# Repeated score passes in head 0's first waits, counting matmuls four steps later, scatters placed 32 score groups later, last stores from two queues

## The reference

```
xn = layernorm(x)
q, k, v = xn @ Wq.T, xn @ Wk.T, xn @ Wv.T          # 16 heads of 16
attn    = softmax(q k^T / sqrt(256)) @ v
rw      = softmax(xn @ gate_w.T), kept for the 2 best of 8 experts (by scores + gate_b)
expert(t) = silu((t @ w1 + b1) * (t @ w3 + b3)) @ w2 + b2      # hidden size 352
out = x + attn + sum_e rw[e] * expert_e(xn) + expert_shared(xn)
```

## Time and profile before

| | |
|---|---|
| three timed runs | 2171.87, 2173.07, 2174.39 us, median 2173.07 |
| the profiled execution | 2174.21 us, of which the span is 2172.3 us |
| busy in the span | PE 99%, ACT 93%, DVE 37%, POOL 11% |
| chain that ended last | PE 92%, ACT 7%, DVE 1% |
| mean granted PE clock | 0.996 of full speed |

### The profile page before, as it was taken

One profiled execution on the slowest core, in us unless ns is written; L12 is line 12 of the kernel. 1 busy time (PEld: TensorE's weight loads), 2 busy tenths in 40 slices (PEclk: granted clock), 3 DMA queues, 4 the chain that ended last, 5 costly groups with the idle time before them and its releaser, 6 DMA issues.

```text
span 2172.3 us, 37982 instructions
## 1 busy us (share of the span) xinstructions
PE 2152.4 (99%) x15638; PEld 965.2 (44%) x15638; DVE 800.5 (37%) x1515; ACT 2009.4 (93%) x2209; POOL 246.0 (11%) x242
## 2 busy tenths in 40 slices
PE   9999999999999999999999999999999999999998
PEld 4632344444444444444444444444444444444322
DVE  6321143344344334334334434334334334544200
ACT  4599999999999999999999999999999999999998
POOL 0100465610000000000000000000000002223200
PEclk9999999999999999999999999999999999999999
DMA  7671334332222222213132222213213222332120
GB/s 254 206 280 33 91 121 130 100 90 66 63 78 63 76 57 79 78 54 85 48 77 70 77 64 69 78 50 83 75 50 90 63 69 75 105 97 66 57 78 3
DMA packets 223595, 187.24 MB, mean 86 GB/s; under 512 B 112039, under 2 KB 194558, under 8 KB 223166
## 3 DMA queue, kind: packets, MB, share of 16 engines
q1 hardware_dynamic: 211598, 149.41, 24.3%
q0 software_dynamic: 11824, 35.40, 5.0%
HBM read 130.21 MB, written 54.53 MB: 85 GB/s over the span
## 4 chain that ended last, share of the span: by engine, by line
PE 92%; ACT 7%; DVE 1%; DMA 0%; issue 0%; DVEq 0%
PE PS L672 41%; PE PS L659 29%; PE PS L684 12%; ACT probs L866 6%; PE PS L695 6%; PE PS L565 2%; PE PS L602 1%; PE PS L575 0%; DVE stats L972 0%; PE PS L554 0%; DMA resid<-in_x 0%; DVE probs L996 0%; ACT probs L818 0%; DVE o_t L1169 0%; DVE mv L975 0%
## 5 line engine op out<-in xcount | busy, mean ns | idle before, releaser
L866 ACT ACTIVATE probs<-PS 128x1024 f32<-128x1024 f32 x2048 | 1920.0, 1080 | 96.0 <-PE PS L659 81.8
L672 PE MATMUL PS<-probs,v_head 128*32 128x512 f32 x8192 | 1002.8, 601 | 1.1 <-ACT probs L866 0.8
L659 PE MATMUL PS<-q_ring,k_stack 50*128 50x512 f32 x4096 | 741.3, 446 | 7.0 <-ACT probs L866 6.2
L659 PEld LDWEIGHTS PS<-q_ring,k_stack 50*128 50x128 f32 x4096 | 332.6, 185 | 627.2 <-ACT probs L866 569.6
L672 PEld LDWEIGHTS PS<-probs,v_head 128*32 128x32 f32 x8192 | 206.6, 108 | 448.2 <-issue 359.6
L1194 DVE TENSOR_SCALAR gate_in<-PS,bias_sb 128x256 f32<-128x256 f32 x165 | 79.6, 482 | 754.9 <-PE PS L684 739.5
L684 PE MATMUL PS<-x_hi,w_hi 128*128 128x256 f32 (+1 forms) x660 | 201.3, 305 | 0.0
L684 PE MATMUL PS<-x_hi,w_lo 128*128 128x256 f32 (+1 forms) x660 | 186.5, 283 | 0.0
L684 PE MATMUL PS<-x_lo,w_hi 128*128 128x256 f32 (+1 forms) x660 | 185.6, 281 | 0.0
L921 POOL DMA_DIRECT2D slot_y<-y_sb x39 | 27.9, 716 | 1285.1 <-DVE y_sb L1262 1251.6
L684 PEld LDWEIGHTS PS<-x_hi,w_hi 128*128 128x128 f32 (+1 forms) x660 | 118.6, 180 | 60.0 <-issue 60.0
(11 more groups left out here) (137 smaller groups left out, 1098.2 us busy)
## 6 DMA issues: line engine op xcount, KB each, us to landing
w_raw<-in_w SPq DMA_DIRECT2D x110, 352.0 KB
k_stack<-qk_parts SPq DMA_DIRECT2D x120, 128.0 KB
w_raw<-in_w SPq DMA_DIRECT2D x55, 256.0 KB
q_ring<-qk_parts SPq DMA_DIRECT2D x384, 32.0 KB
slot_x<-part_a SPq DMA_DIRECT2D x39, 256.0 KB, 2.3
slot_in<-slot_x SPq DMA_DIRECT2D x156, 64.0 KB, 2.4
slot_y<-y_sb POOLq DMA_DIRECT2D x39, 256.0 KB, 2.5
k_stack<-qk_parts SPq DMA_DIRECT2D x136, 64.0 KB
```

The costliest lines, as they stand in the source:

```text
L659: last = pe.matmul(bank(2 * score_buffer(turn, g) + r), k_stack[rows, kt * P:(kt + 1) * P], q_ring[rows, sweep, i * QC:(i + 1) * QC], star ...
L672: last = pe.matmul(bank(O_BANK)[VW * j:VW * (j + 1), :], v_head[:, kt, :], probs[:, slot, (j % 2) * QC:(j % 2 + 1) * QC], start=(kt == 0), ...
L866: nc.scalar.activation(probs[:, prob_slot(g), :], bank(2 * score_buffer(h, g), 2), ACT.Exp, scale=ENERGY_SCALE).then_inc(s_exp, 1)
```

## The change

Four edits. (1) `filler(count)` repeats the first score matmuls of head 0 into banks 6 and 7, whose content nobody reads then; seven such pairs stand between the first score groups. The order of the real score groups and `values` is as before. (2) The counting matmuls stand in step 24 of head 0, not 20. (3) `scatter(u)` waits for `s_scores` at 128 + 32 + 8u, not 128 + 10u. (4) Of the last four stores, two are issued by ACT.

```
-                for c in range(sweep * QCH, (sweep + 1) * QCH):
+                for c in range(sweep * QCH, (sweep + 1) * QCH - 2 * sweep):
...
                 for k in range(1, GS + 1):
+                    if h == 0 and k == 1:
+                        continue
                     next_scores(2)
-                    if h == 0 and k == 20:
+                    if h == 0 and k == 24:
...
+            def filler(count):
+
+                for n in range(count):
+                    for r in range(2):
+                        rows = slice(r * HALF, r * HALF + ROWS)
+                        pe.matmul(bank(F_BANK + r), k_stack[rows, 0:P], q_ring[rows, 0, 0:QC], start=True, stop=True)
+
             next_scores(SB)
+            filler(3)
+            next_scores(1)
+            filler(2)
+            next_scores(1)
+            filler(2)
+            next_values(1)
             plain_head(0)
...
+            act.wait_ge(s_resid, SH + SWEEPS)
+            for c in range(NCH - 2, NCH):
+                nc.scalar.dma_start(out_v[:, c * TPC:(c + 1) * TPC, D - HD:D], resid[:, c * TPC:(c + 1) * TPC, D - HD:D]).then_inc(s_out, 16)
...
                 if u >= 2:
                     pool.wait_ge(s_scat[u % 2], 16 * TPU * TOP * (u // 2))
-                pool.wait_ge(s_scores, GH + 10 * u)
+                pool.wait_ge(s_scores, GH + 32 + 8 * u)
```

## The result

The changed kernel takes 2187.97 us (median of 5 runs, 2186.32 to 2189.01) against 2174.39 us of the kernel before (5 runs, timed beside it): ratio 1.0064, interval 1.0053 to 1.0075. Forecast was 2187.7, counted as 14.6 us over the median of 2173.07 that the kernel before had in its first three runs. The loss is 13.6 us, and the two profiled spans differ by as much (2185.9 against 2172.3).

The account below looks back on a forecast made before the run. PE was taken to bound heads 1 to 14, ACT heads 0 and 15. Edits 1 to 4: -1.8 + 0 + 17.4 - 1.0 = +14.6 us, giving 2187.7 us against the median 2173.07; 8-in-10 range 2176 to 2199.

Parts of the forecast that it names:

- The bound and the reading of POOL: Heads 0 and 15 go at ACT's pace, heads 1 to 14 at PE's; POOL's chain is held by its own work.
- the sharing: Split of the token-wait loss: unit 4 0, unit 5 7.7 us, unit 6 another 7.9, unit 7 nothing more; total 15.6.
- The start: POOL's first scatter, waiting for count 160, starts at 266.5 us instead of 234.03, 32.5 us later.
- Landing: Time a token load of POOL needs to land after its issue: 3.8 us, from 3.0 to 7.5.
- The free lateness: Between DVE's and PE's first use of a unit's tokens, 1.25 us of lateness costs nothing.
- The clock: PE leaves unit 6's token wait with its clock down: +1.8 us; the fall at unit 5 is swallowed.
- the rule of the Trainium skill: Long idle gaps between matmul bursts return PE to half clock; by it both forecast stands, units 5 and 6, bring a fall.
- The fall at 256.5 us: PE clock fall in the profile before, costing ACT 1.76 us; may come or go, left to the range.
- The rival of "another phase": The clock fall around 257 us may come or go, 1.8 us each way; in every range, no chance of its own.
- The chain that catches up: POOL's chain is quicker, 162 us to unit 6's load; -2.8 us, 2170.3; 0.14, shared with POOL being misread.
- The longer chain: POOL's chain gains no 4.4 us and a second clock fall adds 1.8: 2193.9 us; chance 0.20.
- the rule by which both stands' falls are paid in full: Clock falls after the stands at units 5 and 6 both paid: the term would be twice 1.8 us; no chance given.

Follow-up runs that it names:

- the run with the stands filled: Changed kernel plus identity matmuls ahead of up_both(u, 0) of units 4, 5, 6; 2185.49 us against 2170.55 us of the kernel before, ratio 1.0071.

## Why the prediction was right, and where its terms were not

**The bound and the reading of POOL: right.** POOL waited for a score count once (`L904` before, `L923` after), its chain moved as a block, and PE lost in the mixed heads what it waited there.

**Edit 3: right in mechanism and sum (+17.4 forecast, 18.2 in the ledger), by terms that were each a little off.**
- The chain from the first scatter to unit 6's load was to shrink by 4.4 us from 182.2; it shrank by 3.2, to 179.0. The wait of 6.80 us did go (2.37 in its place), and over the 14 scatters POOL waited 4.1 us less for its loads (49.5 against 53.6). But its normalisations and indirect DMAs took 0.9 us more, which the sum didn't have.
- Therefore the sharing was off. Up to unit 4's load the chain had shrunk by 0.5 us only (100.6 to 100.1), where the sum gave it all of the 4.4 at once. Unit 4 was forecast to lose nothing; measured from unit 3's, its split came 4.9 us late and PE stood for 3.22 us. That the total doesn't depend on the sharing, since the last late load sets it, held.
- The start: 262.66 us, with PE 4.4 us ahead of the profile before, is 267.0 on that profile's clock, against 266.5. Landing: 3.2 us for unit 6's load against 3.8.
- The free lateness: 1.25 us counted, 1.1 there. Unit 6's split is 18.0 us late (13.6 and the 4.4 of lead), but PE uses it 1.29 us after it begins instead of 2.38, so PE starts the unit 16.9 us late. The sum had 15.6.
- The clock: +1.8 forecast for the last stand, 1.3 measured: from PE's first use of unit 6's tokens to unit 7's split it was 30.09 us (433.64 to 463.73) and is 31.37 (446.18 to 477.55). So 16.9 + 1.3 = 18.2 stands against 15.6 + 1.8 = 17.4.
- The clock was down behind all three stands, the shortest of which had PE idle for 3.22 us. That is as the rule of the Trainium skill said it would be behind each stand ("TensorE: Matmul & The Clock Gate", "Why this matters for your kernels"). But in the run with the stands filled it fell behind 2.79 us of idle and not behind 3.08.
- That threshold steps of 8 groups don't hold the chain, and that SP's queue would be late without cost: both held. `load_slots(8)` went out at 468.19 us (471.8 forecast), and unit 8's split came 32.33 us after unit 7's. It held also where PE had not slipped: DVE waited 2.74 and 6.85 us for the weights, PE not at all.

**Edit 1: the fall was avoided, the gain isn't shown.** ACT's 1.81 us of idle are gone from the profile. Over all profiles taken, the clock fell at the start in two of two without the passes and in one of twelve with them. That speaks for the passes, though two is few. But the price of 1.8 was read from one profile: in the other without passes (only the new thresholds) the same fall cost ACT 0.61 us. In the medians edit 1 is worth 0.9 us, with an interval from 3.5 us quicker to 0.4 slower: the forecast of 1.8 is inside, and so is nothing.

**The fall at 256.5 us came out in my favour.** It is not in the profile after; by it PE's lead grows from 2.5 us in unit 0 to 4.6 at unit 1's split, 2.1 us, and ACT began head 0 0.5 us sooner. Together with the first fall that is the 4.4 us of the ledger. The rival of "another phase" is real: of the twelve profiles without passes in these places, the clock fell around 254 us in eight and around 2025 in eight. The forecast put it at nothing and left it to the range. Without it and the 0.5 us the spans would differ by 16.2 us, where the sum was 14.6. So it is partly luck that the loss came within 1.0 us of the forecast (13.6 against 14.6), and wholly luck that the two times agree to 0.3 us: the kernel before was 1.3 us slower as timed beside the change than in the runs that the forecast started from.

**Edit 2: right, 0.** DVE's idle ahead of head 0's first output is 4.82 us in the profile after, where the sum left 4.8 of the 12.17. **Edit 4: half.** From the first store's issue to the end of the span it was 3.9 us before and is 3.4 now: -0.5, not -1.0. Two issues on a queue take 0.93 to 1.03 us, but the last landing takes 2.3 us instead of 1.9.

**The rivals.** The chain that catches up fell: it needed 162 us and took 179. The longer chain fell too. So did the rule by which both stands' falls are paid in full: the sharing didn't change the total.

## What to carry to other kernels

Before a wait is moved on an engine that also issues DMAs for others, list everything behind it in that engine's order and take, for each transfer, the time from its issue to its first use: here that was 31.8, 23.0 and 15.1 us against a move of 32.5, and the sum gave the loss before anything ran. If an engine's chain runs back to back, as POOL's did, its thresholds are not what holds it, and moving the first one moves all. The remedy is order, not speed: putting the small urgent load ahead of the long patient work turned a loss of 0.64% into a gain of 0.16%, and another queue for that load did as much (0.15%). And before a wait is priced, see how long the result lies unused: what PE had in hand there (1.1 us) came off the price.

## What the runs showed of the hardware

- The PE clock's falls in thin places come and go between executions: with the same instructions there, a fall showed around 254 us in eight of twelve profiles and not in four. A single profile's fall isn't a property of the kernel, nor is its price: at the start ACT's idle for it was 1.81, 0.61 and 1.07 us in the three profiles that have it.
- A fall behind a stand of 3.4 us cost PE 1.3 to 1.5 us of one unit (32.66 us with the clock down, 31.17 with it up).
- POOL's 256 KB loads of token rows were waited for between 2.3 and 7.3 us; the indirect DMAs took from 0.96 to 2.10 us of POOL each for the same shape. Chains of 14 scatters and four token loads took 173.8 to 182.7 us in the profiles.
